# A fused attention, expert and MLP block on one core: one ring of seven PSUM banks, part loads through DRAM, and expert weights as masked exponentials

## The reference

```python
xn = _layernorm(x)
# attention: 16 heads of 8 features, rotary embedding, causal softmax
qkv = xn @ Wqkv; Q, K = rope(q), rope(k)
scores = jnp.where(causal, Q @ K.T / sqrt(8), min); y = softmax(scores) @ V; out1 = y @ Wproj
# experts: two sub-key similarities per head (4 heads, 64 keys), the 8 best sums
q = (xn @ Wq).reshape(b, t, 2, 4, 64); sim = einsum(q, keys)
sx, sy = top_k(sim[0], 8), top_k(sim[1], 8)
all_sc = sx[..., :, None] + sy[..., None, :]          # 64 sums per head
scores, pk = top_k(all_sc, 8); idx = ixx * 64 + ixy   # 512 experts; larger indices are clipped
w = silu(xn . down_embed[idx]) * softmax(scores); out2 = sum(w * up_embed[idx])
# MLP
out3 = (silu(xn @ Wg + bg) * (xn @ Wu + bu)) @ Wd + bd
return x + out1 + out2 + out3
```

## Time and profile before

| | |
|---|---|
| median of 3 runs | 856.98 us |
| the profiled execution, its own time | 858.98 us |
| its span, first to last instruction | 856.9 us |
| mean granted TensorE clock | 0.936 |
| TensorE, VectorE, ScalarE, GpSimd busy | 756.2, 678.5, 464.6, 539.0 us |
| bytes by DMA | 22.59 MB |

### The profile page before, as it was taken

One profiled execution on the slowest core, in us unless ns is written; L12 is line 12 of the kernel. 1 busy time (PEld: TensorE's weight loads), 2 busy tenths in 40 slices (PEclk: granted clock), 3 DMA queues, 4 the chain that ended last, 5 costly groups with the idle time before them and its releaser, 6 DMA issues.

```text
span 856.9 us, 17118 instructions
## 1 busy us (share of the span) xinstructions
PE 756.2 (88%) x6108; PEld 337.0 (39%) x6108; DVE 678.5 (79%) x1776; ACT 464.6 (54%) x651; POOL 539.0 (63%) x716
## 2 busy tenths in 40 slices
PE   4777698899999998799988999799988998999896
PEld 2433244333443444333443444333433344443332
DVE  3356999878899799987888899986868889987730
ACT  1404222448664863448754863447745685548764
POOL 6515776656766768656657668666645677546850
PEclk9777868999999999989999999979989999999998
DMA  6544002530000003510200002520120000000000
GB/s 129 65 49 61 1 2 38 82 43 15 3 2 30 11 1 47 75 18 1 49 16 15 15 2 33 78 29 1 34 32 2 14 2 1 16 1 1 27 2 13
DMA packets 34608, 22.59 MB, mean 26 GB/s; under 512 B 7260, under 2 KB 34268, under 8 KB 34524
## 3 DMA queue, kind: packets, MB, share of 16 engines
q1 hardware_dynamic: 31324, 20.33, 15.0%
q10 hardware_dynamic: 3200, 1.18, 0.7%
HBM read 6.23 MB, written 2.10 MB: 10 GB/s over the span
## 4 chain that ended last, share of the span: by engine, by line
PE 47%; DVE 23%; POOL 9%; issue 8%; ACT 6%; DMA 3%; SPq 2%; DVEq 0%; POOLq 0%; ACTq 0%
DVE pmax L845 11%; PE ybank L967 9%; PE ring L921 7%; PE ring L1052 6%; PE ring L1042 5%; PE sbank L943 5%; DVE coef L755 5%; PE ring L973 4%; POOL ssum L571 3%; PE ring L1027 2%; SPq L459 2%; PE ring L1034 2%; DMA ks<-parts 2%; POOL coef L618 2%; PE ring L925 1%
## 5 line engine op out<-in xcount | busy, mean ns | idle before, releaser
L845 DVE TENSOR_REDUCE pmax<-ring 128x1 f32<-128x512 f32 (+3 forms) x608 | 371.6, 653 | 76.5 <-PE ring L927 45.1
L719 ACT ACTIVATE pT<-sbank 128x1024 f32<-128x1024 f32 (+3 forms) x384 | 296.5, 809 | 220.6 <-PE sbank L952 108.7
L921 PE MATMUL ring<-ks,qs 48*128 48x512 bf16 (+3 forms) x768 | 205.8, 347 | 37.1 <-DVE pmax L845 16.5
L943 PE MATMUL sbank<-qs,ks 51*128 51x512 bf16 (+3 forms) x768 | 154.7, 345 | 15.4 <-DMA qs<-negmaxT 11.6
L967 PE MATMUL ybank<-pT,vaug 128*32 128x512 f32 (+3 forms) x1536 | 159.9, 517 | 0.0
L571 POOL TENSOR_TENSOR ssum<-sim 128x512 f32<-128x512 f32 x128 | 129.4, 1042 | 42.6 <-DVE coef L755 35.6
L611 POOL TENSOR_TENSOR coef<-exz,edif 128x512 f32<-128x512 f32 x128 | 141.2, 1134 | 2.5
L921 PEld LDWEIGHTS ring<-ks,qs 48*128 48x128 bf16 x768 | 63.4, 95 | 182.9 <-DVE pmax L845 103.0
L755 DVE SCALAR_TENSOR_TENSOR coef<-ssum,best,coef 128x512 f32<-128x512 f32 x128 | 116.3, 933 | 3.5 <-POOL coef L611 3.5
L925 PE MATMUL ring<-step_qk,step_eye 64*128 64x128 bf16 x512 | 97.2, 226 | 0.0
L618 POOL TENSOR_TENSOR coef<-coef 128x1024 f32<-128x1024 f32 x32 | 75.4, 2356 | 29.0 <-DVE coef L755 29.0
(11 more groups left out here) (122 smaller groups left out, 1073.8 us busy)
## 6 DMA issues: line engine op xcount, KB each, us to landing
qs<-parts SPq DMA_DIRECT2D x96, 64.0 KB
ks<-parts SPq DMA_DIRECT2D x96, 64.0 KB
xin<-in_L_attn_x SPq DMA_DIRECT2D x8, 256.0 KB, 3.6
rows<-in_L_attn_x SPq DMA_DIRECT2D x8, 256.0 KB, 3.7
out<-rows SPq DMA_DIRECT2D x8, 256.0 KB, 2.4
qs<-negmaxT SPq DMA_DIRECT2D x32, 12.0 KB
pT<-in_L_ffn_down_embed ACTq DMA_DIRECT2D x1, 256.0 KB, 4.4
pT<-in_L_ffn_Wq ACTq DMA_DIRECT2D x2, 128.0 KB, 5.7
```

The lines of the kernel that those rows point to most:

```text
L719: a_.activation(pT[:, n % NPT, 2 * pr:2 * pr + 2, q0:CHUNK], sbank[:, 2 * pr:2 * pr + 2, q0:CHUNK], ACT.Exp, scale=SCALE).then_inc(probs_r ...
L845: v.tensor_reduce(pmax[:, it, k0 // CHUNK, heads[0]:heads[-1] + 1:2], bank_of(t)[:, 0:w * len(heads)].rearrange("p (h w) -> p h w", w=w), ...
L921: ins = t_.matmul(bank[:, s * w:(s + 1) * w], qs[r, b % 2, h // 2, it * P:(it + 1) * P], ks[r, b % 2, h // 2, k0:k0 + w], start=True, stop ...
L943: ins = t_.matmul(sbank[:, 2 * pr + e, q0:CHUNK], ks[r, b % 2, h // 2, kt * P:(kt + 1) * P], qs[r, b % 2, h // 2, c * CHUNK + q0:(c + 1) * ...
```

## The change

- `NRING` becomes 7 and `sbank` goes. A `scores` task takes two neighbouring banks of the ring, those whose later use ends first; all other tasks take one as before. TensorE waits for the copies of all former users.
- The parts go through a DRAM scratch: one store of a whole piece (`keep_parts`), then six loads per piece instead of twelve, with 24, 16 and 8 partitions of 8 KB each (`TERM_RUNS`). qs and ks are laid out with the chunk ahead of the head pair. `TERMS` has another order, in which equal q parts are neighbours.
- Experts: `near`, the product of two exponentials and `inside` go. `spread` (ScalarE, one per head) is the exponential of the sum less the best score; `keep` (VectorE) turns the sums in place into a mask times one over the softmax sum; `weigh` (GpSimd) multiplies the two; `coef` keeps GpSimd's first sum; `total` (VectorE) does the last sum, with the count from its accumulator, and the correction of expert 511.
- `first`, `second` (casts) and the copy `xT` move from VectorE to ScalarE.
- `SEQUENCE` is another list.

```diff
-TERMS = [(0, 0), (0, 1), (1, 0), (0, 2), (1, 1), (2, 0)]
+TERMS = [(0, 0), (0, 1), (0, 2), (1, 0), (1, 1), (2, 0)]
+TERM_RUNS = [[(0, 3, 0), (3, 2, 1), (5, 1, 2)]] * 2
+NLOADS = 2 * len(TERM_RUNS[0])
-NRING = 3
+NRING = 7
 SEQUENCE = """
-third rot setup*20 second load_parts ln first ropeT expand rest third xn second xT down expand v down rot turned
+ln first setup second rot swapped setup*17 xT first xn second expand keep_parts load_parts down keep_parts gate
...
-            n = min(range(NRING), key=lambda n: -1 if holds[n] is None else ends[holds[n]])
-            bank[key], before[key], holds[n] = n, holds[n], key
+            age = [-1 if use is None else ends[use] for use in holds]
+            if t[0] == "scores":
+                n = min(range(NRING - 1), key=lambda n: max(age[n:n + 2]))
+                bank[key] = [n, n + 1]
+            else:
+                bank[key] = [age.index(min(age))]
+            before[key] = [holds[n] for n in bank[key] if holds[n] is not None]
...
+        parts_dram = nc.dram_tensor("parts_scratch", (2, 3, NC, 2, DH, PAIRS, CHUNK), BF16, kind="Internal").ap()
-        qs = sb("qs", [P, 2, PAIRS, T], BF16)
+        qs = sb("qs", [P, 2, NC, PAIRS, CHUNK], BF16)
...
+                elif kind == "keep_parts":
+                    c, a = t[2:]
+                    sp.wait_ge(parts_ready, piece_no(b, c, a) + 1)
+                    sp.wait_ge(parts_loaded[2 * c + a], 16 * NLOADS * b)
+                    sp.dma_start(parts_dram[a, :, c].rearrange("s h d j t -> (h d j) s t"), parts[:, a, :, :])\
+                        .then_inc(parts_stored[a], 16)
                 elif kind == "load_parts":
-                    sp.wait_ge(parts_ready, piece_no(b, c, a) + 1)
+                    sp.wait_ge(parts_stored[a], 16 * (b * NC + c + 1))
-                    for s, pair in enumerate(TERMS):
-                        for hh in range(2):
+                    for hh in range(2):
+                        for s, n, part in TERM_RUNS[a]:
                             r = HALF * hh + DH * s
+                            if a == 0:
+                                src = parts_dram[a, part, c, hh].rearrange("d j t -> d (j t)").unsqueeze(0)\
+                                    .to_broadcast([n, DH, PAIRS * CHUNK])
+                            else:
+                                src = parts_dram[a, 0:n, c, hh].rearrange("s d j t -> s d (j t)")
+                            sp.dma_start((qs, ks)[a][r:r + DH * n, b % 2, c, :, :].rearrange("r j t -> r (j t)"), src)\
+                                .then_inc(parts_loaded[2 * c + a], 16)
...
-                elif kind == "near":
...
+                    g.tensor_tensor(nbest[:, :], best[:, :, 0], minus[:, :], ALU.mult).then_inc(dif_ready, 1)
-                elif kind == "zinv":
...
+                elif kind == "weigh":
                     for h in range(RH):
+                        pool.wait_ge(kept_ready, RH * i + h + 1)
+                        g.tensor_tensor(coef4[:, h, :], coef4[:, h, :], ssum[:, h, :], ALU.mult).then_inc(weighed, 1)
...
+                elif kind == "spread":
+                    i, h = b * NT + t[2], t[3]
+                    act.wait_ge(dif_ready, 2 * (i + 1))
+                    act.wait_ge(pairs_ready, RH * i + h + 1)
+                    act.wait_ge(coef_ready, i)
+                    a_.activation(coef4[:, h, :], ssum[:, h, :], ACT.Exp, bias=nbest[:, h:h + 1])\
...
                 elif kind == "keep":
-                    v.scalar_tensor_tensor(out=coef4[:, h, :], in0=ssum[:, h, :, :].rearrange("p i j -> p (i j)"),
-                                           scalar=best[:, h, KPH - 1:KPH], in1=coef4[:, h, :],
-                                           op0=ALU.is_ge, op1=ALU.mult, accum_out=inside[:, h:h + 1])\
+                    dve.wait_ge(zinv_ready, i + 1)
+                    dve.wait_ge(spread_ready, RH * i + h + 1)
+                    v.tensor_scalar(ssum[:, h, :], ssum[:, h, :], best[:, h, KPH - 1:KPH], zinv[:, h:h + 1],
+                                    ALU.is_ge, ALU.mult).then_inc(kept_ready, 1)
+                elif kind == "total":
+                    dve.wait_ge(summed, i + 1)
+                    k = steps.mark(v.scalar_tensor_tensor(out=mine, in0=coef4[:, 0, :], scalar=1.0, in1=coef4[:, 1, :],
+                                                          op0=ALU.mult, op1=ALU.add, accum_out=inside[:, :]))
...
-                pe.wait_ge(probs_ready, max(2 * (b * NG + m) + pr - 1, 0))
```

More of the change, by code:

```diff
@@ L199 @@
+scores*2 values*2 ycopy values y yT proj rows outT store
 """
@@ L933, in scores @@
                 c, gr, kt, q0 = EXP_GROUPS[m]
+                banks = pair_of(("scores", b, m, pr))
                 if pr == 0 and m in STAGE_STARTS:
@@ L959, in values @@
                 n = b * NG + m
-                pe.wait_ge(probs_ready, 2 * (n + 1))
+                for pr in range(2):
+                    copied(pe, ("scores", b, m, pr))
                 if m == 0:
```

414 lines of the change are left out of this document (193 added, 221 removed).

## The result

The changed kernel takes 829.38 us (median of 4 runs, 828.72 to 830.49); the kernel before took 857.33 beside it. The ratio is 0.967, 95% interval 0.964 to 0.970: 28 us faster, against a forecast of 828. The total came out as worked out. Where it came from did not.

A forecast was written before the change was run, and what follows sets the result against it. No engine was full; a short queue between nearly equal TensorE and VectorE was taken as the bound. 859.0 - 38 (middle) - 2 (tail) + 7 (start) + 4 (SyncE's order) = 830, as median 828; range 785 to 872.

The forecast's parts named there:

- start +7: First maximum at the start: later part loads cost 12.6 us, partly covered by six more dense matmul tasks; +7 us carried.
- SyncE's order in batch 1 +4: Last k piece in batch 1, issued behind negated-maxima transfers: needs 22 us where 19 are available; +4 us.
- Tail -2: End of the span: masks of the last expert tiles shorten by 0.2 us each, 8 of them; -2 us.
- ScalarE's exponential: Experts on ScalarE: 128 exponentials of 512 columns at 0.60 us each, 77 us in all, bounds 60 and 77.
- mask's price: Experts on VectorE: each in-place mask 0.55 us plus 0.19 waiting for GpSimd, 0.74; 128 of them 95 us.
- rival B: Gain eaten: masks wait out half a GpSimd product each, exponentials hold banks; 861 us, or 854; chance 0.18.
- Against the 58 us of the middle I set 38 us: Middle 700 us: shared ring and lighter VectorE remove two thirds of TensorE's 58 us idle time; -38, bounds 0 and 58.
- the prediction's own signs: Right if TensorE idles near 20 us in the middle; wrong if waits leaving VectorE move to ScalarE's exponentials in equal amount.
- nearly kept: TensorE's task order: 1552 tasks both times, first maxima of batches at 343, 722, 1104 before and 343, 723, 1105 now.
- C: Few DMA engines make part loads slow: 912 us at 33 us a piece, deciding from 22 us; chance 0.15.
- A: TensorE packs: all 58 us idle in the middle go, loads hidden; 797 us, 785 with more overlap; chance 0.17.

The follow-up runs named there:

- the piece moved ahead: Changed kernel with the last k piece's store and loads in batches 1 to 3 issued right behind its last part, ahead of the negated-maxima transfers: 827.37 us.
- faster loads: Changed kernel with the store kept, but each piece loaded from DRAM by twelve transfers of eight partitions instead of six: 816.09 us, then 817.44 us.
- divided banks: Changed kernel with the seven banks divided again: ring tasks only in banks 0 to 2, score pairs only in 3 and 4 or 5 and 6: 912.56 us.
- take out the experts' part: Changed kernel with the experts' weights computed as before, each tile's GpSimd product placed behind the sum of the tile before: 909.21 us.
- kernels of 882, 891 and 909 us: Kernel before with shared seven-bank ring, 881.78 us; changed with twelve DRAM loads, products after all four masks, 890.66; changed with old experts' weights, 909.21.
- short product: Changed kernel with GpSimd's product of experts' weights and mask made for 32 of 512 columns only: 796.64 us.
- all masks first: Changed kernel with twelve DRAM loads, and GpSimd's first product of each tile waiting for all four masks: 890.66 us.

## Why the prediction was right, and where it was not

*The total.* 830 less 2 forecast, 829 measured. The terms: start +7, measured +6 at the first maximum, but only +1 at the first turned one, so the rest of the stage made it up. SyncE's order in batch 1 +4, and this holds: 4 to 6 us by the piece moved ahead, 4.4 by faster loads, nothing in batches 2 and 3. Tail -2: from the 16th turned maximum to the end of the span it was 56.3 us and is 53.0.

*The work per engine.* Within 5 us for VectorE and GpSimd. ScalarE's exponential was mis-sized: 0.717 us where 0.60 was set, 90.0 us in all where the bounds were 60 and 77. I had taken the copy out of a bank as an upper bound for a read from core memory with a bias per partition. The trace of the kernel before had a nearer row, an activation of the same size with such a bias at 0.686:

```profile
L694 ACT ACTIVATE hT<-ring,bg_sb 128x512 f32<-128x512 f32 x32 | 20.7, 686 | 26.8 <-PE ring L1042 26.5
```

That ScalarE still came out below the forecast (545.3, not 558) is no merit of the sum. Its instructions, count times mean, grew by 101 us, more than the 93 forecast, but its busy time only by 81, because 20 us more of them lie over one another. The forecast had no such term, and none for the table loads, which fell by 8. ScalarE had the room in any case. The mask's price was right in both parts (0.550 alone, 0.755 with the port). The Trainium skill's rule on who excludes whom ("SBUF — State Buffer", "Who interferes with whom") says that in such a pair one waits out the whole instruction of the other. The longest mask, 1.565 us, is one of 0.54 behind most of a 1.3 us product; but the median, 0.542, leaves at least half of them undisturbed, so rival B, which had each wait 0.6, is out.

*The step that failed* is "Against the 58 us of the middle I set 38 us". No idle time of TensorE went: 58 before, 65 after. The 28 us came out of its busy time, 642 before and 607 after, which the prediction called "not a hard floor" in passing and then treated as one in the sum. The divided banks show it from the other side: 36.8 us more busy time in the same 768 maximum matmuls. Two of the prediction's own signs say so, too: TensorE was to be idle near 20 us in the middle, and the waits that left VectorE were not to move to ScalarE. Of the 44 us that left, 32 came to ScalarE, and the scores wait for banks that VectorE reads, a hold that the prediction had not named.

*The reason given with it* was incomplete too. VectorE's 19 us and GpSimd's shorter chain were used as weights for one sum. The runs show that ring and experts' part don't add: take out the ring, +83; take out the experts' part, +80; put the ring alone into the old kernel, +20. Nor does TensorE's overlap by itself give the time: it is there in the kernels of 882, 891 and 909 us. The forecast named the order's first maximum tasks (343, 723, 1105) and read from them that the order was "nearly kept". Between these points it is another list: 377 of the 1552 tasks stand at the same place (half of all are moved by at most two places, the farthest by 32), and the maxima stand in 290 groups in place of 374, so more of them follow one another directly. Whether the new kernel lives on that was not tested. That the sum still gave 828 is luck in this step.

*The rivals.* C is out: a piece takes some 15 us (issued at 256.6, used at 271.3), as forecast, below the 22 from which it would have decided. But its mechanism costs 12 us that are there to be had. B's waiting at the port is real, 0.2 us per mask. Without it and without the product's work the kernel takes 33 us less. A did not come: TensorE's idle time stayed. Its "more overlap", which it had priced on top of that, is part of what happened.

*Open:* what the order is worth by itself, and which of its places matter; why the same overlap goes with 829 us in one kernel and with 891 or 909 in others; how the 33 us of the short product divide, since the run that kept the product's work and avoided the meeting changed the product's time as well; and what of each difference is TensorE's clock. The mean granted clock is 0.94 to 0.96 in the kernels near 829, 0.93 in the one with divided banks, 0.91 with all masks first. It does not simply follow idle time: the kernel before has 101 us of it and 0.936, the changed one 108 us and 0.956. No run holds it fixed.

## What to carry to other kernels

Where queues are in order and an order was laid out for one allocation of banks and one set of durations, price the parts of a change together: each alone may lose more than all win. Read a busy TensorE through the mean of one matmul against the group's busy time, since overlap hides in it. When queues come to share banks, look for the waits of each user on every other one, and not only for the wait that was to go. Before a buffer's transfer is replaced, ask who waits for the buffer to come free, and what small transfer stands behind the new one on its engines.

## What the runs showed of the hardware

Twelve DMAs of 64 KB that read DRAM took SyncE 4.0 us to issue, twelve of the same size from core memory to itself 7.9, as these two kernels' rows show. The source differs in its form, too (eight runs of 8 KB each in DRAM, 64 of 1 KB in core memory), so which of the two sets the price is not shown:

```profile
25.07 4.03 SPq L485 DMA_DIRECT2D qs<-parts_scratch  x12
```

```profile
22.70 7.94 SPq L478 DMA_DIRECT2D qs<-parts  x12
```

On ScalarE an exponential of 512 f32 columns from core memory with a bias per partition takes 0.717 us, a cast of 512 from core memory without one 0.625 (line 680 of the changed kernel), and a copy of 512 out of a bank 0.596. GpSimd's product of two plain tensors takes 1.271 us on average where it waits for all masks first and 1.348 where it does not, so GpSimd loses by the meeting as well, but 0.08 us against VectorE's 0.2.
